# A three-layer graph network kernel on one core: who adds the mask to the attention scores in layers 2 and 3

## The chip, the cores and the metric

The kernel runs as one program on one core of a Trainium2 chip. The core has five engines that work side by side and meet only through semaphores: TensorE (PE, with its weight loads shown apart as PEld), VectorE (DVE), ScalarE (ACT), GpSimd (POOL) and SyncE (SP, which issues most DMAs). The metric is the device time of one execution, in microseconds, less is better. A change of under about 0.2% is about what a measurement of this kernel can tell from no change.

## The reference

The input is `x` of 32 x 256 x 256 and an adjacency `adj` of 32 x 256 x 256. Four parts follow one another, each added to `x`: an attention over eight heads, an LSTM over 256 steps, a graph network of three layers, and a product with quantised weights. Only the graph network is touched. For each of its layers l, and each of 32 graphs:

```python
mask = adj + eye(256) > 0
si, sj = x @ attn_w[l, :d], x @ attn_w[l, d:]
scores = si[:, :, None] + sj[:, None, :] + attn_b[l]
scores = where(scores >= 0, scores, 0.2 * scores)
scores = where(mask, scores, -inf)
attn = softmax(scores, axis=-1)
h = layernorm(x + attn @ x) * g1[l] + beta1[l]
ff = gelu(h @ W1[l] + b1[l]) @ W2[l] + b2[l]
x = layernorm(h + ff) * g2[l] + beta2[l]
```

## The kernel before

A graph has 256 nodes, held as two tiles of 128 partitions (NT = 2), with 256 features. `gnn_phase` runs 3 layers x 32 graphs, software-pipelined. `walk` (lines 961 to 975) calls one `body` per graph on every engine, and each engine has its own list of steps, which it works off strictly in order. Within the body of graph b ("now") the engines also work on the next graph ("ahead", b + 1), the one after ("soon", b + 2), the one before ("behind", b - 1) and the one before that ("past", b - 2). The order of the steps inside a `body` is written out by hand.

**Scores and mask.** The score of a pair of nodes is a row term plus a column term. On PE `scores` (line 1611) first multiplies the mask tile `t.gmask` (128 x 512, bf16, 0 or a very large negative number) with the identity into `score_bank` (line 1617), then adds the column term with four products (line 1621). On ACT `slope` (line 1156) writes a relu of the scores into the SBUF tile `slopes` (line 1161), which is what the leaky slope adds. On DVE `largest` (line 1326) adds `score_bank` and `slopes` into `slopes` and takes each row's maximum (line 1331), and line 1336 turns its sign. On ACT `attend` (line 1170) takes the exponential. Each graph's mask is loaded from DRAM into the one tile `t.gmask` by a DMA that ACT issues (`load_mask`, line 1199), right after `slope`.

**The feed-forward part.** PE's `up` (line 1667) multiplies with W1 into four banks, ACT takes the gelu of each bank q (line 1191), and DVE makes from it a rounded upper part and a remainder: `split_act` (line 1394), a CAST in line 1404 and a subtraction in line 1406. In layer 2 ACT makes the upper part of banks 1 and 3 itself (line 1196), in layer 3 that of bank 3 alone. PE's `down` (line 1685) waits for each bank's remainder before it multiplies with W2. `up` and `down` have 48 products each per graph, 12 for each bank. PE's own list for one graph is: `scores` of soon, `up` with `turn_probs` and `aggregate` (line 1638) of ahead in between, `down` of banks 0 to 2, `turn_h` of ahead, `down` of bank 3.

**The second normalisation and GpSimd's list.** POOL's `body` (line 1126) is, in layers 2 and 3: `residual` of now (two multiplications of 128 x 256, line 1076), `rsqrt2` of behind (four tiny steps, lines 1049 to 1054, of which the last releases ACT's `norm2`), in layer 3 `leave` of past (one sum of 128 x 512, line 1116), `residual_end` (two sums, line 1084), `rsqrt1` of ahead, `scale` and `move` of behind (lines 1093 and 1100), and in layer 3 `rsqrt_extra`. ACT's `body` (line 1265) has `norm2` of behind between the gelus of bank 1 and bank 2, so whatever holds back `norm2` holds back the gelus of banks 2 and 3; in layer 3 `norm_extra` (line 1220) lies there too.

Of the kernel before, what the change touches and what calls it, by code (L numbers as in the profile page):

```python
# [11 lines left out]
ALU = mybir.AluOpType  # L12
# [3 lines left out]
P = 128  # L16
B, N, D = 32, 256, 256
# [826 lines left out]
def gnn_phase(nc, t, a, hidden, masks, aside):  # L844
# [5 lines left out]
    with ExitStack() as ctx:  # L850
# [52 lines left out]
        def w1_of(l):  # L903
# [28 lines left out]
            sem(n) for n in ("hg_done", "h_done", "hT_ps", "hT_upper_done", "hT_done", "hidden_ps", "gelu_done", "ff_ps"))  # L932
        w1_upper_done, w1_done, bias_ps, bias_done, ident_done = (
            sem(n) for n in ("w1_upper_done", "w1_done", "bias_ps", "bias_done", "ident_done"))
        sums_done, warm_done = sem("sums_done"), sem("warm_done")
        aside_out, aside_in = sem("aside_out"), sem("aside_in")
        wmost_done, wrow_ps, wrow_done, wtop_ps, wmath_done = (
            sem(n) for n in ("wmost_done", "wrow_ps", "wrow_done", "wtop_ps", "wmath_done"))
# [46 lines left out]
        with nc.Block() as block:  # L985
# [58 lines left out]
            @block.gpsimd  # L1044
            def _(pool):
                def rsqrt(n, mv, veps, minus, rstd, nb, mv_done, veps_done, rstd_done, nb_done):

                    pool.wait_ge(mv_done, n + 1)
                    pool.tensor_tensor(veps[:, :, 0], mv[:, :, 1], t.eps[:, :], ALU.add)
                    pool.tensor_tensor(minus[:, :, 0], mv[:, :, 0], t.minus[:, :], ALU.mult).then_inc(veps_done, 1)  # L1050
                    pool.wait_ge(veps_done, n + 1)
                    pool.tensor_tensor(rstd[:, :, 0], veps[:, :, 0], t.power[:, :], ALU.pow).then_inc(rstd_done, 1)  # L1052
                    pool.wait_ge(rstd_done, n + 1)
                    pool.tensor_tensor(nb[:, :, 0], minus[:, :, 0], rstd[:, :, 0], ALU.mult).then_inc(nb_done, 1)

                def rsqrt1(l, b):
                    rsqrt(l * B + b, mv1, veps1, minus1, rstd1, nb1, mv1_done, veps1_done, rstd1_done, nb1_done)

                def rsqrt2(l, b):
                    rsqrt(l * B + b, mv2, veps2, minus2, rstd2, nb2, mv2_done, veps2_done, rstd2_done, nb2_done)  # L1060

                def rsqrt_extra(n):
                    after(pool, extra_nodes, n)
                    rsqrt(n, mv3, veps3, minus3, rstd3, nb3, extra_mv, extra_veps, extra_rstd, extra_nb)

                def residual(l, b):

                    n = l * B + b
                    if isinstance(b, int) and b == 0:
                        pool.wait_ge(rows_in, (l + 1) * ROWS_IN)  # L1070
                        pool.tensor_tensor(beta1_row[:, :], beta1_row[:, :], b2_row[:, :], ALU.add).then_inc(sums_done, 1)
                        pool.wait_ge(sums_done, l + 1)
                    pool.wait_ge(norm1_done, n + 1)
                    after(pool, r2_done, n)
                    for it in range(NT):
                        last = pool.tensor_tensor(h[:, it, :], r1[:, it, :], g1_row[:, :], ALU.mult)
                    last.then_inc(hg_done, 1)

                def residual_end(l, b):

                    n = l * B + b
                    pool.wait_ge(hg_done, n + 1)
                    for it in range(NT):
                        last = pool.tensor_tensor(h[:, it, :], h[:, it, :], beta1_row[:, :], ALU.add)
                    last.then_inc(h_done, 1)

                def scale(l, b):

                    n = l * B + b
                    alone(pool, norm2_done, n + 1, pool_passed)  # L1090
                    pool.wait_ge(finish_in, (l + 1) * FINISH_IN)
                    for it in range(NT):
                        last = pool.tensor_tensor(t.nodes[:, b, it, :], r2[:, it, :], g2_row[:, :], ALU.mult)
                    last.then_inc(scaled_done, 1)

                def move(l, b):
                    n = l * B + b
                    alone(pool, scaled_done, n + 1, pool_passed)
                    for it in range(NT):
                        last = pool.tensor_tensor(t.nodes[:, b, it, :], t.nodes[:, b, it, :], beta2_row[:, :], ALU.add)  # L1100
                    last.then_inc(nodes_done, 1)

                def enter(e):

                    if isinstance(e, int) and e < 4:
                        pool.wait_ge(hs_first[e], 16)
                    else:
                        pool.wait_ge(hs_in, e * 16 - 48)
                    pool.tensor_tensor(t.x[:, e, :, :], t.x[:, e, :, :], t.nodes[:, e, :, :], ALU.add).then_inc(extra_x, 1)

                def leave(b):

                    pool.wait_ge(nodes_done, (L - 1) * B + b + 1)
                    if isinstance(b, int) and b >= B - LENT:
                        pool.wait_ge(aside_in, 16)
                    pool.tensor_tensor(t.x[:, b, :, :], t.x[:, b, :, :], t.nodes[:, b, :, :], ALU.add).then_inc(extra_x, 1)

                def start(later, soon, at):
                    for e in range(3):
                        enter(e)  # L1120
                        rsqrt_extra(e)
                    enter(3)
                    rsqrt1(*at)
                    rsqrt_extra(3)

                def body(later, soon, ahead, now, behind, past):
                    e, gone = entering(now), leaving(past)
                    residual(*now)
                    if behind:
                        rsqrt2(*behind)  # L1130
                    if e is not None:
                        enter(e)
                    if gone is not None:
                        leave(gone)
                    residual_end(*now)
                    if ahead:
                        rsqrt1(*ahead)
                    if behind:
                        scale(*behind)
                        move(*behind)  # L1140
                    if e is not None:
                        rsqrt_extra(e)
                    if gone is not None:
                        rsqrt_extra(B + gone)

                def end(past, at):
                    leave(past[1])
                    rsqrt2(*at)
                    rsqrt_extra(B + past[1])
                    rsqrt_extra(B + at[1])  # L1150

                walk(pool, start, body, end)

            @block.scalar
            def _(act):
# [42 lines left out]

                def load_mask(l, b):

                    act.dma_start(t.gmask[:, :], masks[(b + 1) % B]).then_inc(gmask_in, 16)

                def norm1(l, b):
# [61 lines left out]
                def body(later, soon, ahead, now, behind, past):  # L1265
                    gone = leaving(past)
                    crossing = ahead and now[0] < ahead[0]
                    if soon:
                        slope(*soon)
                        load_mask(*soon)  # L1270
                    feed(*now, range(0, 2))
                    if behind:
                        norm2(*behind)
                    if later and later[0] == 0:
# [37 lines left out]
            def _(dve):  # L1312
# [13 lines left out]
                def largest(l, b):  # L1326
                    n = l * B + b

                    alone(dve, slopes_done, n + 1, passed)
                    for it in range(NT):  # L1330
                        last = dve.tensor_tensor_reduce(out=slopes[:, it, :], in0=score_bank[:, it * N:(it + 1) * N],
                                                        in1=slopes[:, it, :], scale=1.0, scalar=-3.0e38, op0=ALU.add,
                                                        op1=ALU.max, accum_out=top[:, it:it + 1])
                    last.then_inc(top_done, 1)
                    dve.wait_ge(top_done, n + 1)
                    dve.tensor_scalar(shift[:, :], top[:, :], -1.0, None, ALU.mult).then_inc(shift_done, 1)
# [273 lines left out]
            def _(pe):  # L1610
                def scores(l, b):

                    n = l * B + b
                    pe.wait_ge(parts_done, 2 * n + 2)
                    pe.wait_ge(gmask_in, (n + 1) * 16)
                    after(pe, top_done, n)
                    pe.matmul(score_bank[:, :], t.identb[:, :], t.gmask[:, :], start=True, stop=False,
                              skip_group_check=True)
                    for k in range(2):
                        for jt in range(NT):  # L1620
                            last = pe.matmul(score_bank[:, :].rearrange("p (t s j) -> p t s j", t=NT, s=NT)[:, :, jt, :],
                                             parts[:, k, jt:jt + 1].broadcast_to((P, P)),
                                             t.ident_r[:, :].unsqueeze(1).broadcast_to((P, NT, P)), start=False, stop=True,
                                             skip_group_check=True)
                    last.then_inc(scores_ps, 1)

                def turn_probs(l, b):
# [360 lines left out]
```

## Time and profile before

| | us |
|---|---|
| time, median of 3 runs (lowest, highest) | 2848.49 (2845.19, 2849.57) |
| the profiled execution | 2847.2 |
| its span, first to last instruction | 2845.4 |
| mean granted TensorE clock over the span, of full speed | 0.986 |
| PE matmul busy | 2602.8 (91%) |
| PE weight load busy | 2382.9 (84%) |
| DVE busy | 2054.7 (72%) |
| ACT busy | 1924.7 (68%) |
| POOL busy | 1622.0 (57%) |

The graph network takes the second half: the first scores start at 1257 us and the last of layer 3 end at about 2695 us. The median of the runs lies 1.3 us above the profiled execution, and that lies 1.8 us above its span. Busy shares are averages over parts with different limits, so what a step is worth is read from the stretch where it runs. In the timelines the records of one instruction overlap slightly with the next on the same engine, since an engine starts one while the last results of the one before drain.

### The profile page before, as it was taken

The numbers are of one execution on the slowest core, as the hardware profiler recorded it, in microseconds if no ns is written. First come the engines' busy times: TensorE is split into PE (matmuls) and PEld (weight loads), VectorE is DVE, ScalarE is ACT, GpSimd is POOL, SyncE is SP. The second block draws the span as 40 slices with busy tenths as digits, with TensorE's granted clock in tenths as the row PEclk, the third lists the DMA queues.
The fourth block names the chain that finished last, engine by engine and source line by source line (L and its number), as shares of the span: only waits on it lengthen the run. The fifth ranks groups of instructions, "written<-read, shape, count | busy, mean of one in ns | idle before, by whom it ended". The sixth has DMA issues, their size and how long they took to land. (4 is left out here: it accounts for less than half of the span.)

```text
span 2845.4 us, 117954 instructions
## 1 busy us (share of the span) xinstructions
PE 2602.8 (91%) x44133; PEld 2382.9 (84%) x44228; DVE 2054.7 (72%) x6880; ACT 1924.7 (68%) x5044; POOL 1622.0 (57%) x2673
## 2 busy tenths in 40 slices
PE   7999999978888888869999999999999999999966
PEld 5777777677777777759999999999999999999965
DVE  7999999834444444447777777877777788888888
ACT  4676666744444444438888887788777778888844
POOL 6777777600000000027888885666666677777765
PEclk9999999999999999979999999999999999999989
DMA  3111111000000000020000011100000100000002
GB/s 98 41 37 37 37 37 46 14 11 13 13 13 13 12 13 13 13 79 27 24 26 28 24 37 44 33 9 9 9 7 9 30 31 9 9 7 9 10 15 103
DMA packets 110838, 74.60 MB, mean 26 GB/s; under 512 B 51504, under 2 KB 109360, under 8 KB 110512
## 3 DMA queue, kind: packets, MB, share of 16 engines
q1 hardware_dynamic: 96800, 61.03, 7.5%
q10 hardware_dynamic: 13968, 12.72, 1.5%
q8 instruction: 34, 0.56, 0.1%
q14 instruction: 36, 0.29, 0.0%
HBM read 51.68 MB, written 22.02 MB: 26 GB/s over the span
## 5 line engine op out<-in xcount | busy, mean ns | idle before, releaser
L1679 PE MATMUL g_H<-g_hT_upper,g_w_upper 128*128 128x256 f32 x1536 | 461.4, 300 | 0.2
L1679 PE MATMUL g_H<-g_hT_rest,g_w_upper 128*128 128x256 f32 x1536 | 435.2, 283 | 0.0
L1679 PE MATMUL g_H<-g_hT_upper,g_w_rest 128*128 128x256 f32 x1536 | 434.7, 283 | 0.0
L1707 PE MATMUL g_F<-g_w_upper,g_act_upper 128*128 128x256 f32 x1408 | 410.6, 292 | 8.0 <-DVE g_act_rest L1406 4.8
L1191 ACT ACTIVATE g_act_raw<-g_H,g_small 128x256 f32<-128x256 f32 x768 | 319.5, 471 | 125.0 <-PE g_H L1679 123.9
L762 POOL COPY l_xt<-seq 128x64 f32 x256 | 60.7, 237 | 599.4 <-PE l_O L773 595.8
L1707 PE MATMUL g_F<-g_w_upper,g_act_rest 128*128 128x256 f32 x1408 | 396.0, 281 | 0.0
L1707 PE MATMUL g_F<-g_w_rest,g_act_upper 128*128 128x256 f32 x1408 | 395.1, 281 | 0.0
L334 ACT ACTIVATE a_probs<-a_S,a_nmax 128x256 f32<-128x256 f32 x512 | 237.1, 482 | 105.4 <-DVE a_nmax L432 82.7
L801 ACT ACTIVATE l_ic<-l_G 128x128 f32<-128x128 f32 x256 | 71.1, 278 | 342.0 <-PE l_G L773 342.0
L1406 DVE TENSOR_TENSOR g_act_rest<-g_act_raw,g_act_upper 128x512 fp32r<-128x512 f32 x352 | 267.9, 762 | 46.0 <-ACT g_act_upper L1196 40.4
L1679 PEld LDWEIGHTS g_H<-g_hT_upper,g_w_upper 128*128 128x128 f32 x1536 | 293.8, 191 | 4.1 <-DVE g_hT_rest L1375 1.5
L1679 PEld LDWEIGHTS g_H<-g_hT_rest,g_w_upper 128*128 128x128 f32 x1536 | 294.1, 192 | 2.5
L1679 PEld LDWEIGHTS g_H<-g_hT_upper,g_w_rest 128*128 128x128 f32 x1536 | 293.9, 191 | 0.0
L1707 PEld LDWEIGHTS g_F<-g_w_upper,g_act_upper 128*128 128x128 f32 x1408 | 265.5, 189 | 22.1 <-DVE g_act_rest L1406 21.7
L1707 PEld LDWEIGHTS g_F<-g_w_upper,g_act_rest 128*128 128x128 f32 x1408 | 265.4, 188 | 0.0
L1707 PEld LDWEIGHTS g_F<-g_w_rest,g_act_upper 128*128 128x128 f32 x1408 | 265.3, 188 | 0.0
L773 PE MATMUL l_G<-wh,l_hT 128*32 128x128 f32 x4096 | 165.3, 279 | 106.8 <-DVE l_hT L835 106.2
L820 DVE SCALAR_TENSOR_TENSOR l_fresh<-l_ic 128x64 f32<-128x64 f32 x256 | 57.8, 226 | 277.8 <-ACT l_ic L801 277.8
L1052 POOL TENSOR_TENSOR g_small<-g_small,eps_power 128x2 f32<-128x2 f32 x256 | 219.2, 856 | 20.0
L432 DVE CUSTOM_DVE_ANT_0 a_S<-a_S,a_mask 128x256 f32<-128x256 f32 x512 | 200.0, 458 | 29.7 <-PE a_S L614 25.8
L773 PEld LDWEIGHTS l_G<-wh,l_hT 128*32 128x32 f32 x4096 | 96.6, 109 | 147.9 <-DVE l_hT L835 147.9
(239 smaller groups left out, 8128.7 us busy)
## 6 DMA issues: line engine op xcount, KB each, us to landing
gmask<-masks ACTq DMA_DIRECT2D x97, 128.0 KB, 2.0
x<-in_x_dram SPq DMA_DIRECT2D x32, 256.0 KB, 3.1
a_adj<-in_adj_dram SPq DMA_DIRECT2D x32, 256.0 KB, 2.8
hidden<-l_hs SPq DMA_DIRECT2D x512, 16.0 KB, 1.4
seq<-hidden SPq DMA_DIRECT2D x32, 256.0 KB, 2.7
out_dram<-q_res SPq DMA_DIRECT2D x32, 256.0 KB, 2.1
masks<-gmask SPq DMA_DIRECT2D x32, 128.0 KB, 1.7
g_w_raw<-in_L_gnn_W_dram SPq DMA_DIRECT2D x6, 512.0 KB, 4.0
```

Of the source, the lines that this page charges most:

```text
L334: last = act.activation(probs[h % PROBS][:, it, :], score_bank[h % HG][:, it * N:(it + 1) * N], ACT.Exp, scale=-1.0, bias=nmax[:, h, it:it ...
L432: last = dve.tensor_tensor_reduce(out=score_bank[h % HG][:, part], in0=score_bank[h % HG][:, part], in1=mask[i][:, part], scale=1.0, scala ...
L762: pool.tensor_copy(xt[i][:, :, :], t.seq[:, :, s * 2 + i, :]).then_inc(xt_done, 1)
L773: last = pe.matmul(bank[j * B:(j + 1) * B, 0:(gates.stop - gates.start) * HQ], x[:, c, :], w[:, c, gates, j * HQ:(j + 1) * HQ], start=Fals ...
L801: act.activation(ic[:, :, :], ic_bank[u % 2][:, 0:2 * HQ], ACT.Tanh).then_inc(ic_done, 1)
L820: dve.scalar_tensor_tensor(out=fresh[:, :], in0=ic[:, 0, :], scalar=1.0, in1=ic[:, 1, :], op0=ALU.add, op1=ALU.mult)
L1052: pool.tensor_tensor(rstd[:, :, 0], veps[:, :, 0], t.power[:, :], ALU.pow).then_inc(rstd_done, 1)
L1191: last = act.activation(act_raw[:, 2 * q + i, :], hidden_bank[q][:, i * N:(i + 1) * N], ACT.Gelu, bias=b1_shifted[:, 2 * q + i:2 * q + i + 1])
L1406: dve.tensor_tensor(act_rest[:, span, :], act_raw[:, span, :], act_upper[:, span, :].bitcast(F32), ALU.subtract).then_inc(act_done, 1)
L1679: last = pe.matmul(hidden_bank[m // 2][:, m % 2 * N:(m % 2 + 1) * N], w[:, c, m * P:(m + 1) * P], x[:, c, :], start=(c == 0 and k == 0), s ...
L1707: last = pe.matmul(ff_bank[:, it * D:(it + 1) * D], x[:, m, it * P:(it + 1) * P], w[:, m, :], start=(m == 0 and it == 0 and k == 0), stop= ...
```

## The change

In layers 2 and 3 PE no longer multiplies the mask with the identity, and the first column product starts the bank. In its place GpSimd gets a new step `cover`, first in its body: it waits for `slope` and for the mask's DMA, and adds the mask (bf16) to `slopes` in place, 128 x 512 in one instruction. `largest` on DVE waits for `cover` instead of `slope`. The mask's next load on ACT waits for `cover`, and stands behind the gelus of banks 0 and 1 instead of right behind `slope`. In layer 3 POOL's `leave` moves from behind `rsqrt2` to ahead of it. Layer 1 keeps its work and order.

```diff
+                def cover(l, b):
+
+                    n = l * B + b
+                    alone(pool, slopes_done, n + 1, pool_passed)
+                    pool.wait_ge(gmask_in, (n + 1) * 16)
+                    pool.tensor_tensor(slopes[:, :, :].rearrange("p t n -> p (t n)"), slopes[:, :, :].rearrange("p t n -> p (t n)"),
+                                       t.gmask[:, :], ALU.add).then_inc(covered, 1)
...
                 def body(later, soon, ahead, now, behind, past):
                     e, gone = entering(now), leaving(past)
+                    if soon and soon[0] > 0:
+                        cover(*soon)
                     residual(*now)
+                    if gone is not None:
+                        leave(gone)
                     if behind:
                         rsqrt2(*behind)
                     if e is not None:
                         enter(e)
-                    if gone is not None:
-                        leave(gone)
                     residual_end(*now)
...
                 def load_mask(l, b):
 
+                    if l > 0:
+                        act.wait_ge(covered, (l - 1) * B + b + 1)
                     act.dma_start(t.gmask[:, :], masks[(b + 1) % B]).then_inc(gmask_in, 16)
...
                     if soon:
                         slope(*soon)
+                        if soon[0] == 0:
+                            load_mask(*soon)
+                    feed(*now, range(0, 2))
+                    if soon and soon[0] > 0:
                         load_mask(*soon)
-                    feed(*now, range(0, 2))
...
-                    alone(dve, slopes_done, n + 1, passed)
+                    if l == 0:
+                        alone(dve, slopes_done, n + 1, passed)
+                    else:
+                        alone(dve, covered, n - B + 1, passed)
...
                     pe.wait_ge(parts_done, 2 * n + 2)
-                    pe.wait_ge(gmask_in, (n + 1) * 16)
+                    if l == 0:
+                        pe.wait_ge(gmask_in, (n + 1) * 16)
                     after(pe, top_done, n)
-                    pe.matmul(score_bank[:, :], t.identb[:, :], t.gmask[:, :], start=True, stop=False,
-                              skip_group_check=True)
+                    if l == 0:
+                        pe.matmul(score_bank[:, :], t.identb[:, :], t.gmask[:, :], start=True, stop=False,
+                                  skip_group_check=True)
...
-                                             t.ident_r[:, :].unsqueeze(1).broadcast_to((P, NT, P)), start=False, stop=True,
-                                             skip_group_check=True)
+                                             t.ident_r[:, :].unsqueeze(1).broadcast_to((P, NT, P)),
+                                             start=(l > 0 and k == 0 and jt == 0), stop=True, skip_group_check=True)
```

## Rows read from the trace of the kernel before

**Rows 1.** Windows, layers 2, 3: stretch, length, busy PE, PEld, DVE, ACT, POOL, clock, DMA.

```profile
1760.00:2160.00 400.00, 398.71 (x3111) 389.06 (x3136) 307.82 (x965) 317.25 (x646) 260.55 (x428) 1.00 0.06 16
2300.00:2650.00 350.00, 349.70 (x2715) 338.76 (x2738) 299.50 (x795) 287.79 (x585) 272.63 (x493) 1.00 0.03 9
```

**Rows 2.** Timeline of PE, layer 3: start, duration, engine, line, operation, operands.

```profile
2420.36 0.19 PEld L1707 LDWEIGHTS g_F<-g_w_upper,g_act_upper 128*128 128x128 f32 x1 [0.18 <-DVE g_act_rest L1406]
...
2425.05 0.28 PE L1707 MATMUL g_F<-g_w_rest,g_act_upper 128*128 128x256 f32 x1
2425.21 0.82 PE L1621 MATMUL g_S<-ident_r,g_parts 128*128 128x256 f32 x4
2425.86 0.28 PE L1679 MATMUL g_H<-g_hT_upper,g_w_upper 128*128 128x256 f32 x1
```

**Rows 3.** Timeline of ACT, one graph of layer 3 and the next slope.

```profile
2411.20 0.47 ACT L1161 ACTIVATE g_slopes<-g_S,g_small 128x256 f32<-128x256 f32 x1 [0.54 <-PE g_S L1621]
...
2411.57 0.47 ACT L1161 ACTIVATE g_slopes<-g_S,g_small 128x256 f32<-128x256 f32 x1
...
2413.35 0.84 ACT L1191 ACTIVATE g_act_raw<-g_H,g_small 128x256 f32<-128x256 f32 x2
...
2415.50 1.09 ACT L1214 ACTIVATE g_r<-g_r,g_small 128x256 f32<-128x256 f32 x2 [0.24 <-POOL g_small L1054]
...
2417.58 0.84 ACT L1191 ACTIVATE g_act_raw<-g_H,g_small 128x256 f32<-128x256 f32 x2
...
2426.14 0.47 ACT L1161 ACTIVATE g_slopes<-g_S,g_small 128x256 f32<-128x256 f32 x1 [0.53 <-PE g_S L1621]
```

**Rows 4.** Timeline of DVE, the same graph of layer 3.

```profile
2414.22 0.43 DVE L1404 CAST g_act_upper<-g_act_raw 128x512 fp32r<-128x512 f32 x1 [0.30 <-ACT g_act_raw L1191]
2414.69 0.69 DVE L1406 TENSOR_TENSOR g_act_rest<-g_act_raw,g_act_upper 128x512 fp32r<-128x512 f32 x1
...
2416.10 0.70 DVE L1336 TENSOR_SCALAR g_small<-g_small 128x2 f32<-128x2 f32 x1
...
2419.61 0.70 DVE L1406 TENSOR_TENSOR g_act_rest<-g_act_raw,g_act_upper 128x512 fp32r<-128x512 f32 x1
...
2420.69 0.69 DVE L1406 TENSOR_TENSOR g_act_rest<-g_act_raw,g_act_upper 128x512 fp32r<-128x512 f32 x1
...
2422.13 1.24 DVE L1406 TENSOR_TENSOR g_act_rest<-g_act_raw,g_act_upper 128x512 fp32r<-128x512 f32 x1
```

**Rows 5.** Timeline of POOL, the same graph of layer 3.

```profile
2411.74 1.43 POOL L1076 TENSOR_TENSOR g_h<-g_r,g_g_row 128x256 f32<-128x256 f32 x2 [0.20 <-issue]
2414.01 0.19 POOL L1049 TENSOR_TENSOR g_small<-g_small,eps_power 128x2 f32<-128x2 f32 x1 [0.83 <-DVE g_small L1434]
...
2415.28 0.19 POOL L1054 TENSOR_TENSOR g_small<-g_small 128x2 f32<-128x2 f32 x1
2415.49 1.28 POOL L1116 TENSOR_TENSOR x<-x,seq  x1
...
2421.39 1.44 POOL L1093 TENSOR_TENSOR seq<-g_r,g_g_row 128x256 f32 x2
```

**Rows 6.** Timeline of POOL, DVE and PE, near the end of layer 3.

```profile
2699.89 1.28 POOL L1116 TENSOR_TENSOR x<-x,seq 128x512 f32<-128x512 f32 x1
...
2699.91 1.81 DVE L1406 TENSOR_TENSOR g_act_rest<-g_act_raw,g_act_upper 128x512 fp32r<-128x512 f32 x1
...
2706.47 0.39 PE L1707 MATMUL g_F<-g_w_upper,g_act_upper 128*128 128x256 f32 x1 [1.69 <-DVE g_act_rest L1406]
```

**Rows 7.** Groups of POOL: line, operation, count, busy us and mean ns, idle before.

```profile
L1817 POOL TENSOR_TENSOR q_wq<-q_wsum,q_wstep 128x512 bf16<-128x512 f32 x1 | 1.5, 1452 | 0.1
```

**Rows 8.** Timeline of ACT and DVE, one graph of layer 2.

```profile
2016.21 0.48 ACT L1161 ACTIVATE g_slopes<-g_S,g_small 128x256 f32<-128x256 f32 x1 [0.45 <-PE g_S L1621]
...
2019.24 0.43 DVE L1404 CAST g_act_upper<-g_act_raw 128x512 fp32r<-128x512 f32 x1 [0.29 <-ACT g_act_raw L1191]
...
2030.92 0.48 ACT L1161 ACTIVATE g_slopes<-g_S,g_small 128x256 f32<-128x256 f32 x1 [0.45 <-PE g_S L1621]
```

More of the change, by code:

```diff
@@ L934, in gnn_phase @@
             sem(n) for n in ("w1_upper_done", "w1_done", "bias_ps", "bias_done", "ident_done"))
-        sums_done, warm_done = sem("sums_done"), sem("warm_done")
+        sums_done, warm_done, covered = sem("sums_done"), sem("warm_done"), sem("covered")
         aside_out, aside_in = sem("aside_out"), sem("aside_in")
```

## Prediction, made before the changed kernel was run

> **What bounds the kernel now.** I read the profile in this order: the busy windows of each layer, the timeline of PE through one graph, then that of the engines that feed it. The windows [rows 1] show PE's matmuls busy for 398.7 of 400 us in layer 2 and 349.7 of 350 us in layer 3, at full granted clock. No other engine comes near in layer 2 (DVE 308, ACT 317, POOL 261 of 400), but in layer 3 DVE is busy 299.5 of 350 us and POOL 272.6. So PE's own list sets the pace, and each 0.1 us taken off it is worth up to 0.1 us per graph, as long as nothing else is late. Two things are nearly late. In layer 3 PE's load for bank 1 of the second product waits 0.18 us for DVE's remainder [rows 2]: from one slope to the next a graph takes 2426.14 - 2411.20 = 14.94 us [rows 3], in layer 2 it is 2030.92 - 2016.21 = 14.71 us [rows 8]. So in layer 3 the pace is really set by a chain through all engines: scores on PE, slope, gelu of bank 0 on ACT, then DVE's unbroken list down to bank 1's remainder, then PE's second product and the next scores. In layer 2 ACT waits 0.45 us for PE at each slope [rows 8]; that is all the slack that ACT's own ring has.
>
> **PE: what is removed.** The mask product's own records are missing from the trace, so it is worked out from its neighbours. From the last g_F product (2425.05) to the first g_H product (2425.86) are 0.81 us [rows 2]. In it lie one g_F product and four score products. Products of 256 columns follow each other every 0.12 us: from the load at 2420.36 to the product at 2425.05 lie 35 spacings and four short transposes, for which I take 0.5 us off, so (4.69 - 0.5) / 35 = 0.12. Five of them are 0.6, which leaves 0.21 us for the mask product; twice the spacing, for its 512 columns, would be 0.24. I take 0.215 per graph. 64 graphs x 0.215 = 13.8 us, all on PE, all of it on the path if nothing else is late. This is the whole possible gain. PE's wait for the mask DMA goes too; it ended nothing.
>
> **POOL: what is added, `cover`.** It is one 128 x 512 sum of f32 and bf16. The nearest row is `leave`, same size, both inputs f32: 1.28 us [rows 5]. The bounds are one 128 x 256 step below (half of 1.43 = 0.72 us, as if bf16 cost nothing), and 1.45 us above, the one 512-wide sum with a bf16 side, there the output [rows 7]. I take 1.28. It can't start before slope is done. All times from here are counted from the start of slope, at 2411.20. Slope ends at 2411.57 + 0.47, so at 0.84; with a hop of 0.08 to 0.1 us `cover` runs from 0.93 to 2.21. POOL's `residual` ran from 0.54 to 1.97 [rows 5]; it now runs from 2.24 to 3.67, in two halves that meet at 2.96. DVE's `largest`, which now waits for `cover`, comes only at 4.1 (after bank 0's remainder, 2414.69 + 0.69 - 2411.20 = 4.18 [rows 4]), so the wait itself is hidden.
>
> **What `residual` and `leave` now meet.** The cost is not the wait but where the big POOL steps fall. In layer 3 DVE's two-column L1336 takes 0.70 us from 2416.10, up to 2416.80 [rows 4], and the POOL sum L1116 beside it ran from 2415.49 to 2416.77 [rows 5]: it stood until POOL was through. A remainder L1406 at 2422.13 takes 1.24 instead of 0.69 us, under the second half of L1093 (2421.39 to 2422.83): 2422.83 + 0.54 = 2423.37, its end [rows 4, 5]. And once near the end of the layer L1116 started at 2699.89, 0.02 us ahead of a remainder: that remainder took 1.81 us, to 1.28 + 0.55 after L1116's start, and PE then waited 1.69 us for the next one (a graph whose gelu was late as well) [rows 6]. So a large POOL step and these DVE steps exclude each other for the whole step.
>
> The Trainium skill, "SBUF — State Buffer", section "Who interferes with whom", states the same as a rule: casts and tensor_scalar in a two-port mode, and sums with both inputs in SBUF, take an exclusive pair of ports that GpSimd also needs, and whoever comes second stands until the first is through. The trace agrees by the three rows just named. By that page's rule this change, which moves large GpSimd work into the middle of these DVE steps, costs time; without the rule it would give the 13.8 us.
>
> **Layer 3.** DVE's CAST for bank 0 is issued at 2414.22, at 3.02. `residual`'s second half now lies over it, 2.96 to 3.67. The CAST gets through at 3.67 + 0.3 = 3.97 instead of 3.45 (its 0.43 us less the start-up). Meanwhile `leave`, now right behind `residual`, stands ready from 3.67 and takes the ports as the CAST lets go; it then holds them for about 1.1 us (1.28 less some 0.2 of start), to 5.06. Bank 0's remainder, issued at 4.00, ends at 5.06 + 0.54 = 5.60 instead of 4.18: 1.42 late. `largest` follows, and L1336 now comes when POOL has only tiny steps, so its stretch of 0.70 - 0.17 = 0.53 us is given back. What is behind it is 1.42 - 0.53 = 0.9 us late: the aggregated sum, its moments, and the remainder of bank 1 (before at 2419.61 + 0.70, so 9.11), which PE already waits for [rows 2]. So the graph's time is 14.94 + 0.9 - 0.21 = 15.63 us: 0.69 more. `leave` runs in 30 of the 32 graphs: 30 x 0.69 = 20.7 us.
>
> A second path gives a floor to this, also if the order slips. `rsqrt2` started at 2.81 and released ACT's norm2 at 4.27 [rows 5]. Behind norm2 on ACT's list stand norm_extra and the gelus of banks 2 and 3: gelu 2 ended 3.0 us after that release (2417.58 + 0.84 = 7.22) [rows 3], and bank 2's remainder, which now ends at 2420.69 + 0.69 = 10.18 [rows 4], can't come sooner than a CAST and a subtraction, 1.15 us, after gelu 2. Now `rsqrt2` comes after `leave` and after the late remainder, 5.6 + 1.35 = 6.95. Gelu 2 ends at 9.95 and bank 2's remainder at 11.1; PE comes to it 12 products (1.42 us) after bank 1, at 9.16 + 1.42 = 10.58 before and 11.5 now. Just hidden here.
>
> **Layer 2.** There is no `leave`. The CAST comes at 2019.24 - 2016.21 = 3.03 [rows 8], under the same half of `residual`, and is 0.5 us late. Behind it come tiny steps only, so nothing is added. The 0.5 us travels through the aggregated sum, the first root on POOL, norm1, a table load, the upper part of hT and the exponential to the next slope. That ring had 0.45 us of slack [rows 8], so it takes 14.71 - 0.45 + 0.5 = 14.76 to 14.78 us: 0.06 more, though PE needs 0.21 less. 32 x 0.06 = 1.9 us. The mask's DMA (issue of 0.35 us on ACT's queue) stands now behind the gelu of bank 1 and lies beside an upper part or norm2; it has over 10 us to land. I cost it at nothing; if its cover is gone it would be 0.35 us per graph, 11 us a layer.
>
> **Sum.** Layer 3 +20.7, layer 2 +1.9: +23 us on the profiled execution (span 2845.4 to 2868; 2847.2 to 2870). The median stands 1.3 us above that execution: 2848.5 + 23 = 2871.5 us.
>
> **Rivals.**
> (1) *The gain is kept.* The big POOL steps pass DVE without a meeting that matters, and PE gets 0.2 us in each graph. For it speaks that PE is busy all the time and that the ends meet within 0.06 us (CAST at 3.02, half at 2.96). Against it, that there is a CAST or a remainder from 3.02 to 4.18 without a break, while POOL has 2.7 us of big steps after 2.2. It gives 2848.5 - 13 = 2835.5 us, down to 2834.7 and up to 2839 if layer 3 keeps PE's wait.
> (2) *`cover` is longer, 1.36 us or more.* Then the CAST slips in between `residual`'s halves, the second half delays the remainder by about 0.5 us, `leave` starts at about 4.5 and ends at 5.6, so L1336 is stretched as before and bank 1 isn't late. But `rsqrt2` ends at 7.1, gelu 2 at 10.1, and bank 2's remainder at 11.3 where PE wants it at 10.6: 0.7 - 0.21 = 0.5 per graph, 15 us, and layer 2 as above. 2865.5 us. It decides from a `cover` of 1.35 us.
> (3) *`cover` is short, near 0.72 us.* `residual` then ends at 3.1, the CAST loses 0.1, the remainder 0.9, L1336 gives 0.5 back: layer 3 +0.14 x 30 = +4, layer 2 keeps its 0.2 x 32 = -6. About 2846.5 us.
> (4) *POOL becomes the bound in layer 3.* It is busy 272.6 of 350 us, 11.6 us per graph, and gets 1.28 more, and its steps stand as well when DVE has the ports, some 0.5 each for three of them. Its `residual_end` would then end at 8.4 or later and meet bank 1's CAST at 8.9. If that adds 0.5 us per graph: 2887 us. It decides once `residual_end` ends after 8.9.
>
> **Chances.** My sum 0.40; rival 2 0.16; rival 4 0.08; rival 1 0.22; rival 3 0.14 (half of it within 0.2%, a quarter to each side). The predicted time is that of the sum. The three slow cases alone span 2858 to 2890; the unknown price of `cover` and rival 1 pull the low end down to 2836. Range 2836 to 2886. Within 0.2% (5.7 us, about what a measurement of this kernel can tell from no change): 0.07; faster 0.26; slower 0.67.
>
> **What would show it.** In layer 3's steady part: the distance between slopes 15.6 us (rival 1: 14.75; rival 2: 15.4), bank 0's CAST stretched to about 0.95 us and its remainder to about 1.6 us, L1336 back at 0.17, PE waiting some 1.0 us at the load for bank 1's remainder; `cover` at 1.28 us, starting 0.93 after slope; norm2 about 7 us after slope. In layer 2: 14.77 us between slopes, PE waiting for the hT remainder, ACT no longer waiting for PE at slope. From the last g_F to the first g_H 0.6 us where hT is not late. A `cover` far from 1.28, or a POOL step that gives way to the DVE steps, would make it wrong.

## The result and the profile after

The changed kernel takes 2858.84 us (median of 5 runs, 2857.18 to 2865.14) where the kernel before takes 2845.19 us (median of 5, 2844.23 to 2849.57): a ratio of 1.0048, 95% interval 1.0035 to 1.0062. It is 0.5% slower. The prediction was 23 us slower, the runs say 13.7. (The predicted 2871.5 us also stood on 2848.5 us for the kernel before, 3.3 more than its median here.) The profiled execution of the changed kernel has a span of 2863.2 us, 17.8 more than before; it is the slowest of its five runs.

The windows of the same stretches as in [rows 1] (length, busy PE, PEld, DVE, ACT, POOL, clock, DMA, GB/s) show where PE no longer keeps up:

```profile
1760.00:2160.00 400.00, 396.19 (x3104) 385.14 (x3104) 314.21 (x960) 318.99 (x643) 296.72 (x453) 1.00 0.06 17
2300.00:2650.00 350.00, 335.03 (x2604) 322.51 (x2603) 306.74 (x764) 270.73 (x563) 295.87 (x495) 1.00 0.03 8
```

PE was busy 349.7 of 350 us in layer 3 and is now busy 335.0. The waits of 2330 to 2660 us, in layer 3 (engine, line, what it waited for, us in total, times, longest), say on what:

```profile
ACT g_r L1226 <- POOL g_small L1054: 54.7, 21, 2.6
...
PEld g_F L1727 <- DVE g_act_rest L1424: 17.9, 21, 0.9
...
PE g_F L1727 <- DVE g_act_rest L1424: 13.5, 21, 0.7
```

Once per graph PE stands up to 0.9 us before a remainder of DVE (its weight load and its product wait for the same one), and ACT's norm2 stands 2.6 us before POOL's root.

I count time between starts of slope, one per graph and 96 in all, and cut the span where the pace changes: 23 steady graphs of layer 2, 25 of layer 3, and the turns between layers (6 graphs, then 8). The first of the 25 still belongs to the turn (15.38 us before, 15.70 after); the other 24 take 14.95 and 15.59 us.

| us | to slope 32 | turn 1-2 | layer 2 (per graph) | turn 2-3 | layer 3 (per graph) | rest |
|---|---|---|---|---|---|---|
| before | 1726.2 | 98.6 | 338.6 (14.72) | 127.8 | 374.3 (14.97) | 180.0 |
| after | 1729.1 | 96.4 | 340.9 (14.82) | 124.9 | 390.0 (15.60) | 182.0 |
| difference | +2.9 | -2.2 | +2.3 | -2.9 | +15.7 | +2.0 |

The 2.9 us ahead of slope 32 are not the change's, since the work on every engine is the same there up to then; it is the spread between executions (in the profiles of all eleven kernels of this document this stretch lies between 1722.3 and 1729.1 us). The loss is layer 3's. The turns, which I had not counted, give back 5.1 us.

One steady graph of layer 3 after, on POOL, DVE, PE's loads and ACT (start, duration, engine, line, operands; the two slopes frame it, and lines have moved: CAST L1422, remainder L1424, sign L1354, `cover` L1071, `residual` L1084, `leave` L1124):

```profile
2416.06 0.84 ACT L1171 ACTIVATE g_slopes<-g_S,g_small 128x256 f32<-128x256 f32 x2 [0.29 <-PE g_S L1641]
...
2422.93 1.10 ACT L1226 ACTIVATE g_r<-g_r,g_small 128x256 f32<-128x256 f32 x2 [2.60 <-POOL g_small L1054]
...
2425.36 0.70 DVE L1424 TENSOR_TENSOR g_act_rest<-g_act_raw,g_act_upper 128x512 fp32r<-128x512 f32 x1
...
2426.11 0.19 PEld L1727 LDWEIGHTS g_F<-g_w_upper,g_act_upper 128*128 128x128 f32 x1 [0.84 <-DVE g_act_rest L1424]
...
2431.65 0.84 ACT L1171 ACTIVATE g_slopes<-g_S,g_small 128x256 f32<-128x256 f32 x2 [0.30 <-PE g_S L1641]
...
2432.74 1.16 POOL L1071 TENSOR_TENSOR g_slopes<-g_slopes,gmask 128x512 f32<-128x512 f32 x1 [0.50 <-ACT g_slopes L1171]
2433.86 1.44 POOL L1084 TENSOR_TENSOR g_h<-g_r,g_g_row 128x256 f32<-128x256 f32 x2
2435.24 1.46 POOL L1124 TENSOR_TENSOR x<-x,seq  x1
...
2434.67 0.90 DVE L1422 CAST g_act_upper<-g_act_raw 128x512 fp32r<-128x512 f32 x1
2435.61 1.64 DVE L1424 TENSOR_TENSOR g_act_rest<-g_act_raw,g_act_upper 128x512 fp32r<-128x512 f32 x1
...
2437.97 0.17 DVE L1354 TENSOR_SCALAR g_small<-g_small 128x2 f32<-128x2 f32 x1
```

Read the DVE rows against POOL's. The CAST of bank 0 (0.43 us in [rows 4]) takes 0.90: it is held until `residual` is through. `leave` then waits for the CAST (1.46 instead of 1.28 us) and holds the remainder: it ends at 2437.25, 0.55 us after `leave` (2436.70). The sign step (L1354), once 0.70 us [rows 4], is back at 0.17. This is what `leave` did once near the end of the layer before the change [rows 6], now in every graph.

### The profile page after: what moved, and what is told of

Read it like the earlier page. It is cut to its first block and busy times, and to the rows that moved or that the text cites. A ratio compares the mean times of both kernels' runs of the same rounds, so it can differ in the third digit from the quotient of the medians.

```text
span 2863.2 us, 118168 instructions
## 1 busy us (share of the span) xinstructions
PE 2601.0 (91%) x44133; PEld 2379.6 (83%) x44164; DVE 2083.9 (73%) x6880; ACT 1919.8 (67%) x5044; POOL 1709.7 (60%) x2737
## 5 line engine op out<-in xcount | busy, mean ns | idle before, releaser
L1727 PE MATMUL g_F<-g_w_upper,g_act_upper 128*128 128x256 f32 x1408 | 409.6, 291 | 24.0 <-DVE g_act_rest L1424 20.7
L1424 DVE TENSOR_TENSOR g_act_rest<-g_act_raw,g_act_upper 128x512 fp32r<-128x512 f32 x352 | 290.3, 825 | 46.1 <-ACT g_act_upper L1206 40.3
L1699 PEld LDWEIGHTS g_H<-g_hT_upper,g_w_upper 128*128 128x128 f32 x1536 | 293.8, 191 | 15.6 <-issue 7.3
```

The source lines that it names most:

```text
L1424: dve.tensor_tensor(act_rest[:, span, :], act_raw[:, span, :], act_upper[:, span, :].bitcast(F32), ALU.subtract).then_inc(act_done, 1)
L1699: last = pe.matmul(hidden_bank[m // 2][:, m % 2 * N:(m % 2 + 1) * N], w[:, c, m * P:(m + 1) * P], x[:, c, :], start=(c == 0 and k == 0), s ...
L1727: last = pe.matmul(ff_bank[:, it * D:(it + 1) * D], x[:, m, it * P:(it + 1) * P], w[:, m, :], start=(m == 0 and it == 0 and k == 0), stop= ...
```

## The experiments

Each is compared with runs of the kernel before on the same chip; the paces are those of the table above.

| kernel | median us | ratio to before (95%) | layer 2 | layer 3 |
|---|---|---|---|---|
| changed | 2858.84 | 1.0048 (1.0035 to 1.0062) | 14.82 | 15.60 |
| leave behind again | 2837.68 | 0.9972 (0.9961 to 0.9983) | 14.80 | 14.84 |
| no mask product, no cover | 2833.20 | 0.9956 (0.9939 to 0.9972) | 14.51 | 14.72 |
| leave ahead only | 2838.94 | 0.9978 (0.9968 to 0.9987) | 14.72 | 14.72 |
| cover second | 2827.10 | 0.9933 (0.9917 to 0.9950) | 14.76 | 14.51 |
| root first in layer 2 | 2855.52 | 1.0030 (1.0020 to 1.0039) | 15.64 | 14.51 |
| leave in halves | 2860.68 | 1.0046 (1.0029 to 1.0063) | 14.81 | 15.58 |
| mask twice | 2845.50 | 0.9994 (0.9985 to 1.0004) | 14.85 | 15.07 |
| cover second, pair early | 2827.75 | 0.9945 (0.9930 to 0.9960) | 14.62 | 14.51 |
| pair early only | 2846.64 | 1.0005 (0.9995 to 1.0015) | 14.72 | 14.97 |

**1. One part undone: `leave` behind the root.**

```diff
                     residual(*now)
-                    if gone is not None:
-                        leave(gone)
                     if behind:
                         rsqrt2(*behind)
+                    if gone is not None:
+                        leave(gone)
```

> The changed kernel with one part undone: in layer 3 leave stands behind rsqrt2 again; cover stays first. My theory (the large POOL step leave stands on bank 0's remainder on DVE): that remainder falls from 1.64 to about 0.7 us, the CAST stays near 0.9, norm2's release comes 5.5 us after slope, and the time from slope to slope in layer 3 falls from 15.60 to about 15.0 us (residual_end then brushes bank 1's CAST). Layer 2 stays at 14.82. In all some 16 us less than the changed kernel, about 2843 to 2846. Rival (cover itself, as 1.2 us more work in POOL's list, is the cost): layer 3 stays at 15.4 us or more, the time within 5 us of the changed kernel's.

Measured 2837.7 us, 21 less than the changed kernel and 7 less than before; layer 3 14.84. The same steps in layer 3:

```profile
2408.43 0.90 DVE L1422 CAST g_act_upper<-g_act_raw 128x512 fp32r<-128x512 f32 x1
2409.36 0.70 DVE L1424 TENSOR_TENSOR g_act_rest<-g_act_raw,g_act_upper 128x512 fp32r<-128x512 f32 x1
2410.78 0.17 DVE L1354 TENSOR_SCALAR g_small<-g_small 128x2 f32<-128x2 f32 x1
...
2410.92 1.29 POOL L1124 TENSOR_TENSOR x<-x,seq  x1
```

The CAST is still held by `residual` (0.90), the remainder is free (0.70 instead of 1.64), and `leave` starts 0.14 us behind the sign step. The order of `leave`, 1.3 us of work that was there before, decides between 0.5% slower and 0.3% faster. With it here, moving the mask to GpSimd is a small gain. But this run undoes two things at once: the remainder is free, and the root comes earlier, so that norm2 starts 5.52 us after slope instead of 6.87. It doesn't part the two; experiment 6 does. My figure of 15.0 for layer 3 was 0.16 too high; bank 1's CAST stands under `residual_end` as expected, but by 0.15 us only (0.55 instead of 0.40).

**2. What the product is worth on PE.** Line 1617 in layers 2 and 3 is left out, with nothing in its place, so these scores carry no mask; the first column product starts the bank (that line is left out below).

```diff
-                    pe.matmul(score_bank[:, :], t.identb[:, :], t.gmask[:, :], start=True, stop=False,
-                              skip_group_check=True)
+                    if l == 0:
+                        pe.matmul(score_bank[:, :], t.identb[:, :], t.gmask[:, :], start=True, stop=False,
+                                  skip_group_check=True)
...
```

> The kernel before without its mask product in layers 2 and 3, and nothing in its place: the mask is left out of the computation there, so it shows what PE's product is worth alone. My theory: 0.21 us per graph, 14.50 us from slope to slope in layer 2 and 14.74 in layer 3, where the chain through DVE keeps its length; with the turns between layers 14 to 18 us less than before, about 2829 to 2833. Rival (in layer 3 DVE's chain alone sets the time): layer 3 stays at 14.95, and only some 8 us are gained.

Layer 2 goes from 14.722 to 14.506, layer 3 from 14.970 to 14.723: 0.22 and 0.25 us per graph, and in all 11.9 us. The paces are as expected, the total is less than the 14 to 18 that I had: the turns and the end gain next to nothing (turn 2-3 127.8 in both). So 0.21 to 0.22 us was the right price, but not for all 64 graphs.

**3. The other part alone: `leave` ahead of the root in the kernel before.**

```diff
                     residual(*now)
+                    if gone is not None:
+                        leave(gone)
                     if behind:
                         rsqrt2(*behind)
-                    if gone is not None:
-                        leave(gone)
```

> The kernel before with leave ahead of rsqrt2 in layer 3 and nothing else. POOL then has residual from 0.54 to 1.97 us after slope and leave from 1.97 to about 3.2. My theory: bank 0's CAST (3.02) waits 0.2 us for leave, its remainder follows without a wait, and L1336 loses its stretch of 0.5 us, so bank 1's remainder is 0.3 us earlier and PE's wait of 0.18 us there is gone: 14.75 to 14.80 us from slope to slope in layer 3, 4 to 6 us less than before, about 2840. Rival (leave ahead of the root costs by holding back norm2): layer 3 goes up to 15.1 us or more, 4 us slower.

2838.9 us, 0.2% faster than before, layer 3 14.72. Each of the two parts gains 6 to 7 us by itself (`cover` in place of the product 7 us in experiment 1, `leave` ahead of the root 6 us here), and both together lose 13.7. Alone, `leave` ahead of the root lies over little:

```profile
2408.06 1.29 POOL L1116 TENSOR_TENSOR x<-x,seq  x1
...
2409.44 0.48 DVE L1404 CAST g_act_upper<-g_act_raw 128x512 fp32r<-128x512 f32 x1 [0.29 <-ACT g_act_raw L1191]
2409.96 0.69 DVE L1406 TENSOR_TENSOR g_act_rest<-g_act_raw,g_act_upper 128x512 fp32r<-128x512 f32 x1
2411.37 0.17 DVE L1336 TENSOR_SCALAR g_small<-g_small 128x2 f32<-128x2 f32 x1
```

`leave` ends as the CAST starts, and the sign step (L1336) loses the stretch that it had before the change [rows 4]. Put `cover` in front of it, and it slides by 1.2 us onto the remainder.

**4. All of POOL's work, in an order that misses DVE's steps.**

```diff
-                    if soon and soon[0] > 0:
-                        cover(*soon)
                     residual(*now)
-                    if gone is not None:
-                        leave(gone)
+                    if soon and soon[0] > 0:
+                        cover(*soon)
                     if behind:
                         rsqrt2(*behind)
                     if e is not None:
                         enter(e)
                     residual_end(*now)
+                    if gone is not None:
+                        leave(gone)
```

> The changed kernel with another order on POOL: residual, cover, rsqrt2, residual_end, leave. residual runs from 0.54 to 1.97 us after slope, cover from 1.97 to 3.1, the tiny steps over bank 0's CAST and remainder, residual_end over L1336 as leave was before, leave between 6.3 and 7.6, before bank 1's CAST at 8. My theory (what costs is a large POOL step over a DVE step with two SBUF inputs or in a fast mode, not POOL's amount of work): the CAST loses 0.1 us, nothing else is late, 14.5 to 14.55 us in layer 2 and 14.8 to 14.85 in layer 3; about 14 us less than before, 2831 to 2834, the fastest of all. Rival (POOL is full in layer 3 with cover added): 15.2 us or more in layer 3, not faster than before.

2827.1 us: the fastest of all, 0.7% faster than before and 32 us faster than the changed kernel with the same instructions. Layer 3 runs at 14.51 and PE is busy there all the time (310.00 of 310 us from 2330 to 2640), so this is PE's own list. POOL, busy 282 of these 310 us, holds nothing back. Layer 3 of this run:

```profile
2401.30 1.42 POOL L1084 TENSOR_TENSOR g_h<-g_r,g_g_row 128x256 f32<-128x256 f32 x2 [0.20 <-issue]
2402.68 1.17 POOL L1071 TENSOR_TENSOR g_slopes<-g_slopes,gmask 128x512 f32<-128x512 f32 x1
...
2407.07 1.29 POOL L1124 TENSOR_TENSOR x<-x,seq  x1
...
2403.73 0.43 DVE L1422 CAST g_act_upper<-g_act_raw 128x512 fp32r<-128x512 f32 x1 [0.29 <-ACT g_act_raw L1201]
2404.19 0.70 DVE L1424 TENSOR_TENSOR g_act_rest<-g_act_raw,g_act_upper 128x512 fp32r<-128x512 f32 x1
2405.61 0.17 DVE L1354 TENSOR_SCALAR g_small<-g_small 128x2 f32<-128x2 f32 x1
```

`cover` ends at 2403.85, 0.12 us into the CAST, and the next big step starts at 2405.68. Layer 2 missed the forecast (14.76, not 14.5): there `residual` waits for the sum `g_r` on DVE until 1.0 us after slope and not 0.5, and `cover` lies on the CAST again (0.73 to 0.90 us instead of 0.43).

**5. Another order for layer 2: cover, root, residual.**

```diff
+                    early = covering and now[0] < L - 1
+                    if early:
+                        cover(*soon)
+                        rsqrt2(*behind)
                     residual(*now)
...
```

Left out are the lines that give all other bodies the order of experiment 4.

> As the kernel with cover second in layer 3, and in layer 2 another order on POOL: cover, rsqrt2, residual, residual_end. There cover lies from 0.93 to 2.1 us after slope, the root's tiny steps over bank 0's CAST and remainder (3.0 to 4.2), residual from about 4.3 to 5.7. My theory: the CAST is back at 0.43 us, the aggregated sum, which needs residual to be through, is 0.3 us late instead of 0.6, and ACT's ring lets layer 2 go down from 14.76 to 14.5 to 14.6 us; layer 3 stays at 14.51. 2821 to 2824 us. Rival (what keeps layer 2 at 14.76 is cover's 1.2 us in the way from slope to the maximum, not where residual and cover lie): layer 2 stays within 0.05 us of 14.76, 2827 us.

A clear miss: layer 2 goes to 15.64. The CAST is indeed back at 0.40 us, but the aggregated sum waits for POOL:

```profile
2029.77 1.02 POOL L1052 TENSOR_TENSOR g_small<-g_small,eps_power 128x2 f32<-128x2 f32 x1
...
2031.03 1.43 POOL L1084 TENSOR_TENSOR g_h<-g_r,g_g_row 128x256 f32<-128x256 f32 x2
...
2032.74 0.88 DVE L1381 SCALAR_TENSOR_TENSOR g_r<-g_A,g_small,seq 128x256 f32<-128x256 f32 x2 [1.54 <-POOL g_h L1084]
```

I had `residual` through at 5.7 us after slope; it is at 6.4, since the root starts later (3.25) and is itself held by the CAST and the remainder (its third step, first row, takes 1.02 us; at 2437.52 in the changed kernel it takes 0.70). The exclusion works in both directions, and I had priced it in one.

**6. `leave` in halves, in the changed kernel.**

```diff
-                    pool.tensor_tensor(t.x[:, b, :, :], t.x[:, b, :, :], t.nodes[:, b, :, :], ALU.add).then_inc(extra_x, 1)
+                    for it in range(NT):
+                        last = pool.tensor_tensor(t.x[:, b, it, :], t.x[:, b, it, :], t.nodes[:, b, it, :], ALU.add)
+                    last.then_inc(extra_x, 1)
```

> The changed kernel with leave as two sums of 128 x 256 in place of one of 128 x 512, everything in its place. POOL then needs about 0.15 us more for it. My theory (DVE stands until the one POOL instruction in flight is through, and the two engines take turns): bank 0's remainder falls from 1.64 to about 1.1 us, L1354 stays at 0.17, bank 1's remainder is 0.5 us earlier, and layer 3 goes from 15.60 to 15.1 to 15.2 us, 11 to 13 us less than the changed kernel, about 2847. Rival (POOL's amount of work and the late release of norm2 set the time): layer 3 at 15.6 us or above.

Half right:

```profile
2414.40 2.06 POOL L1125 TENSOR_TENSOR x<-x,seq  x2
...
2414.77 1.10 DVE L1426 TENSOR_TENSOR g_act_rest<-g_act_raw,g_act_upper 128x512 fp32r<-128x512 f32 x1
...
2417.84 1.10 ACT L1228 ACTIVATE g_r<-g_r,g_small 128x256 f32<-128x256 f32 x2 [2.97 <-POOL g_small L1054]
```

The remainder falls from 1.64 to 1.10 us, as said: DVE stands for one POOL instruction and then gets its turn between the halves (`leave` now lasts 2.06). But the mean pace stays at 15.58. It is made of two kinds of graphs: of the 24 steady ones, 11 take 15.3 us and 13 take 15.8.

In the graph of these rows, one of 15.3 us, the late root is the bound. ACT's norm2 starts 7.02 us after slope (2410.82), and from there ACT's list runs without a gap to the next slope at 2426.13, 8.29 us later: 15.31 in all. So the late root alone would hold layer 3 at 15.3.

The graphs of 15.8 us hold another meeting. First bank 2's remainder in a graph of 15.8 us, with `scale` of POOL and PE's wait, then the same two steps in the graph of 15.3 us:

```profile
2405.34 1.88 POOL L1101 TENSOR_TENSOR seq<-g_r,g_g_row 128x256 f32 x2
2405.36 1.27 DVE L1426 TENSOR_TENSOR g_act_rest<-g_act_raw,g_act_upper 128x512 fp32r<-128x512 f32 x1
...
2406.68 0.19 PEld L1729 LDWEIGHTS g_F<-g_w_upper,g_act_upper 128*128 128x128 f32 x1 [0.66 <-DVE g_act_rest L1426]
```

```profile
2421.14 0.69 DVE L1426 TENSOR_TENSOR g_act_rest<-g_act_raw,g_act_upper 128x512 fp32r<-128x512 f32 x1
...
2421.84 1.44 POOL L1101 TENSOR_TENSOR seq<-g_r,g_g_row 128x256 f32 x2
```

In all 13 graphs of 15.8 us `scale` starts some 0.02 us ahead of the remainder, which then takes 1.27 us, and PE waits 0.66 us for it; in all 11 of 15.3 us the remainder comes first and takes 0.69. My 15.1 to 15.2 us missed both kinds. The rival's number came true (15.6 us), but only half of its reason: the late root gives 15.3, and it pushes bank 2's remainder to where `scale` can slip in ahead of it.

**7. `cover` added, the product kept.** The kernel of experiment 1 with line 1617 and its wait back in layers 2 and 3, so the mask is added twice.

> cover added on POOL, leave behind rsqrt2 as before, and PE keeps its mask product as well, so the mask is added twice. Against the run with leave behind and no product (layer 2 14.80, layer 3 14.84 us) it shows what PE's product is worth once cover is there. My theory (with cover there, ACT's and DVE's rings set the pace, not PE): layer 2 14.8 to 14.9, layer 3 14.85 to 14.95, that is 1 to 5 us more than that run, 2839 to 2843 us. Rival (PE's list still counts in full): 0.21 us per graph more, 15.0 and 15.05 us, 13 us more, 2851 us.

2845.5 us, between theory and rival. With `cover` there, the product costs 0.05 us per graph in layer 2 (14.80 to 14.85), where other rings set the pace, and its full 0.23 in layer 3 (14.84 to 15.07). In all it is 7.8 us by the medians, or 6.4 once the 1.4 us are taken off by which the kernel before was slower on this run's chip.

**8 and 9. The second row sum earlier in layer 2**, with cover second, and alone in the kernel before.

```diff
+                    both = pairing and not crossing and not entered and l == 1
                     if pairing and not crossing and not entered:
                         next_pair(*past, 0)
+                    if both:
+                        next_pair(*past, 1)
...
-                    if pairing:
+                    if pairing and not both:
                         next_pair(*past, 1)
```

> The kernel with cover second, and in layer 2 DVE takes both row sums of the next pair (line 1440's operation) ahead of the hT remainder, where it waits 2 us for ACT, instead of one ahead and one behind. In that kernel's layer 2 residual waits for DVE's r2 until 1.0 us after slope, since r2 stands behind the second row sum (0.7 us), and so cover lies over bank 0's CAST until 3.5. My theory: residual starts at 0.35 to 0.6, cover ends by 3.1, the CAST falls from 0.82 to under 0.5 us, and layer 2 goes from 14.76 to 14.5 to 14.55 us, PE's own list; layer 3 stays at 14.51. 2820 to 2823 us. Rival (the row sums, which have two SBUF inputs, now stand under scale and move on POOL and hold back the hT remainder): layer 2 at 14.75 or above, 2827 us or more.

> Control: the kernel before with only that move of the second row sum in layer 2. PE's list alone sets layer 2 there (14.72 us), so the move should change nothing: 14.72 us in layer 2, within 2 us of the kernel before in all. If it gains more than 4 us, the gain of the run beside it is the move's and not that of the two together.

The CAST is back at 0.43 us, and layer 2 falls from 14.76 to 14.62, short of the 14.5 to 14.55 that I had: the graphs run from 14.47, PE's own list, to 14.72, and what holds the slower ones is open. Alone the move does nothing to the pace (14.72). The total missed too: it stays at 2827.75. The steady graphs win 3.3 us and the turns lose 5.6 (turn 1-2 96.3 to 98.6, turn 2-3 123.9 to 127.2).

## Why the prediction was right, and where its sizes were off

**The sign and the mechanism held.** In layer 3, forecast and measured: slope to slope 15.63 and 15.60; CAST about 0.95 and 0.90; bank 0's remainder about 1.6 and 1.64; sign step 0.17 and 0.17; the end of bank 1's remainder at 9.11 + 0.9 and 10.00 (2425.36 + 0.70 - 2416.06); PE's wait about 1.0 and 0.84; norm2 about 7 and 6.87 after slope. In layer 2 14.77 and 14.82, the CAST at 0.85 to 0.92 us; and ACT, which waited 0.45 us for PE at each slope, now waits 0.15 us at most. The changed kernel and experiments 1 and 4 do the same work in three orders and take 2859, 2838 and 2827 us, so the cause is where POOL's steps lie and not how much they are. That the held remainder sets the pace in the changed kernel is read from PE's wait there; experiment 6 shows that freeing it alone gains nothing, since `leave` ahead of the root also delays norm2, and that path is only 0.3 us shorter.

The Trainium skill, "SBUF — State Buffer", section "Who interferes with whom", says that between GpSimd and such a DVE step the second to come waits until the first is through. The rows agree each time: 1.64 us under a whole `leave`, 1.10 under half of one, 0.70 with none.

**Misses that cancelled.** `cover` takes 1.16 to 1.18 us, not 1.28, but starts 1.09 us after slope, not 0.93. It ends at 2.25 where I had 2.21, and so `residual`'s halves lie as forecast (the second starts at 2.90, the CAST comes at 3.02). That is luck in part: the hop from ACT to POOL was 0.25 us and not 0.08 to 0.1, and with it a `cover` of the 1.28 us that I took would have put the second half at about 3.02, the edge where rival 2 (a late half) begins. It didn't come: the CAST stands until the second half is through. Rival 3 (a short cover) fell with the 1.16 us.

**The terms that were mis-sized.** The sum was 23 us; the runs say 13.7, and the profiled execution, once the 2.9 us ahead of the change are taken off, 15.
- Layer 3 was 30 x 0.69 = 20.7. The trace has bank 0's remainder at 1.64 us in 25 graphs, not 30, and these graphs are 0.64 us longer each (15.59 against 14.95 in the steady ones): 16.0 us. The graph on either side of them adds 0.3, and what follows adds 1.0: 17.7 in all. So the step was sized a little high, and the graphs at the layer's ends, where `leave` runs but doesn't meet the remainder, were counted in full.
- Layer 2 was 1.9 and is 2.3.
- The turns were counted as nothing, or as layer 2's 0.06; this is the largest part of the miss. They give 5.1 us back. In nine graphs of the two turns before the change, the sign step stood under `residual_end` (0.75 to 0.76 us; first two rows, before); after it, it stands in none (third row):

```profile
2228.31 1.44 POOL L1084 TENSOR_TENSOR g_h<-g_h,g_beta_row 128x256 f32<-128x256 f32 x2
2229.02 0.76 DVE L1336 TENSOR_SCALAR g_small<-g_small 128x2 f32<-128x2 f32 x1
```

```profile
2230.80 0.17 DVE L1354 TENSOR_SCALAR g_small<-g_small 128x2 f32<-128x2 f32 x1
```

The last three graphs of layer 2 went from 15.1 to 15.7 us down to 14.5 to 14.8. Experiments 2, 3 and 9, which leave `cover` out, keep the nine long sign steps, and their turn 2-3 stays at 127.8. The changed kernel and experiments 1, 4, 6 and 7 have none and take 123.6 to 124.9. Experiments 5 (127.8) and 8 (127.2) have `cover` and lose the gain: there six graphs of the turns have the sign step at 0.76 us again. So the gain goes with the order on POOL and DVE and with the sign step in each of the eleven traces, though no run tests that step by itself. The move of experiment 8 is paid for here as well: in it an early graph of layer 2 takes 16.48 us (14.80 in experiment 4), and it takes 16.48 in experiment 9 too (15.40 before).
- The second path (norm2 late) was called "just hidden", with bank 2's remainder as its end. It is hidden, as said (15.2 to 15.3 us under the 15.6 that DVE's chain asks for: norm2 at 6.87, and 8.29 from there to the next slope in experiment 6), but its end is ACT's list. Experiment 6 uncovered it.

**Rival 1** (the gain is kept, 13 us) fell for this order. Experiment 2 shows the product's worth, 11.9 us; experiment 4 gains 18, with an order that also frees the sign step in layer 3 (0.17 us) and in the turns. **Rival 4** (POOL the bound) fell with experiment 4, and in the changed kernel `residual_end` ends 8.23 us after slope, ahead of bank 1's CAST at 8.86.

## What to carry to other kernels

Before a step goes to GpSimd, lay its interval, and those of all GpSimd steps that it pushes back, over the DVE casts, tensor_scalar steps and sums with two SBUF inputs of one steady period; where two meet, the later one waited out the whole instruction in every row here, and what counts is whether DVE's step feeds the bound engine. Two changes that each gain can lose together when one slides the other onto such a step, so an order should be tried again after each. A step's duration in the trace that is twice its usual one, with a GpSimd row ending just before it does, is the sign to look for, and a gap-free list behind a late release (here ACT's behind norm2) gives the floor that a repair of the first cause can't pass. A mean pace can hide two kinds of periods: where two steps are ready within 0.02 us of each other, list the periods one by one.

## What the runs showed of the hardware

- On GpSimd a 128 x 512 sum with f32 and bf16 inputs takes 1.16 us, against 1.28 for two f32 inputs.
- The two engines take turns: while DVE stands behind one GpSimd instruction, it gets through before the next one of GpSimd's queue (remainder 1.10 us between the halves of `leave`, which then last 2.06 us, and 1.27 us between the halves of `scale`, which then last 1.88), and a waiting GpSimd step gets in between two DVE steps (`leave` between CAST and remainder).
- The steps that stood were casts, tensor_scalar and sums with two SBUF inputs. The maximum step with one input in PSUM (L1331, L1349) stayed at 0.41 to 0.42 us, and in the kernel before it ran under `leave` (2415.30 to 2416.06 against 2415.49 to 2416.77).
- GpSimd's small steps stand as well: the third step of the root, two columns, takes 0.70 us in the changed kernel (2437.52) and 1.02 us beside the remainder in experiment 5.
